# Two factor projections of a four-layer kernel: high and low halves of the weights side by side in one stationary tile

## The reference, cut to what matters

```
a = x @ Wa                      # [4, 512, 16]: one factor per token and head
b = x @ Wb                      # the same
for s in range(4):              # lags 0 to 3
    attn = einsum('bshd,bshd->bsh', q, lag(k, s)) * scale
    gate = sigmoid(lag(a, s) * b)
    out += (attn * gate)[..., None] * lag(v, s)
```

## Time and profile before

| | us |
|---|---|
| median of 3 runs | 2850.12 (2850.07 to 2850.35) |
| span of the profiled execution | 2847.8 |
| PE busy in that span | 2826.6 (99%) |
| DVE busy | 2252.7 (79%) |
| ACT busy | 1528.7 (54%) |
| POOL busy | 1443.2 (51%) |

### The profile page before, as it was taken

How to read it: one execution, slowest core, us unless ns; L and a number is a source line. 1 busy time by engine, 2 the same in 40 slices (tenths; PEclk the granted TensorE clock), 3 DMA queues, 4 the chain that set the end, 5 groups by cost and what they waited for, 6 DMA issues and landing times. The chain is left out here.

```text
span 2847.8 us, 40066 instructions
## 1 busy us (share of the span) xinstructions
PE 2826.6 (99%) x13466; PEld 2348.4 (82%) x13466; DVE 2252.7 (79%) x3265; ACT 1528.7 (54%) x3149; POOL 1443.2 (51%) x1016
## 2 busy tenths in 40 slices
PE   9999999999999999999999999999999999999998
PEld 7888888888788888888888888778778887888887
DVE  7899587777888889888988898977667677666665
ACT  6656333333666666666666666765545445444443
POOL 7787233334344444444444444666545556555554
PEclk9999999999999999999999999999999999999999
DMA  3000000000322222222222221321111111211111
GB/s 138 1 23 25 12 19 27 30 27 23 125 65 68 70 64 64 65 73 64 64 64 72 77 71 53 93 75 52 52 45 52 60 45 56 86 45 60 52 52 45
DMA packets 79099, 160.44 MB, mean 56 GB/s; under 512 B 11313, under 2 KB 19889, under 8 KB 77873
## 3 DMA queue, kind: packets, MB, share of 16 engines
q1 hardware_dynamic: 78896, 157.88, 18.5%
HBM read 115.63 MB, written 8.65 MB: 44 GB/s over the span
## 5 line engine op out<-in xcount | busy, mean ns | idle before, releaser
L1546 DVE SCALAR_TENSOR_TENSOR x_tok<-OP,expert_weight,x_tok 128x512 f32<-128x512 f32 x252 | 188.1, 748 | 138.2 <-PE OP L47 138.1
L1425 POOL TENSOR_TENSOR middle_w_lo<-second_raw,middle_w_hi 128x512 fp32r<-128x512 f32 (+1 forms) x96 | 143.4, 1496 | 208.7 <-ACT middle_w_hi L1420 208.7
L1518 POOL TENSOR_TENSOR middle_in_lo<-middle_slot,middle_in_hi 128x512 fp32r<-128x512 f32 x128 | 168.6, 1318 | 131.7 <-ACT middle_in_hi L1514 130.9
L3017 POOL TENSOR_TENSOR lag_rnorm<-lag_norm,minus_half 128x8 f32<-128x8 f32 x64 | 105.1, 1643 | 209.5 <-DVE lag_norm L3408 209.5
L45 PE MATMUL B<-xT_hi,lag_w_hi 128*128 128x512 f32 x516 | 201.4, 390 | 1.8 <-DVE xT_lo L496 1.5
L47 PE MATMUL B<-xT_hi,lag_w_lo 128*128 128x512 f32 x516 | 201.6, 391 | 0.0
L45 PE MATMUL A<-xT_hi,lag_w_hi 128*128 128x512 f32 x512 | 200.6, 392 | 0.4 <-DVE xT_lo L496 0.4
L46 PE MATMUL B<-xT_lo,lag_w_hi 128*128 128x512 f32 x516 | 200.8, 389 | 0.0
L47 PE MATMUL A<-xT_hi,lag_w_lo 128*128 128x512 f32 x512 | 199.9, 390 | 0.0
L46 PE MATMUL A<-xT_lo,lag_w_hi 128*128 128x512 f32 x512 | 199.4, 389 | 0.0
L45 PE MATMUL OP<-middle_down_hi,middle_in_hi 128*128 128x512 f32 x496 | 193.6, 390 | 1.9 <-POOL middle_down_lo L1445 1.7
(11 more groups left out here) (670 smaller groups left out, 9103.8 us busy)
## 6 DMA issues: line engine op xcount, KB each, us to landing
lag_raw<-in_head_weights SPq DMA_DIRECT2D x64, 256.0 KB, 4.5
lag_b_row<-lag_b_scratch SPq DMA_DIRECT2D x64, 256.0 KB, 3.3
lag_rot_q<-lag_r SPq DMA_DIRECT2D x128, 128.0 KB, 2.3
lag_rot_k<-lag_r SPq DMA_DIRECT2D x128, 128.0 KB, 2.4
middle_down_raw<-in_expert_down SPq DMA_DIRECT2D x32, 512.0 KB, 3.4
middle_raw<-in_expert_in SPq DMA_DIRECT2D x32, 384.0 KB, 3.0
second_raw<-in_expert_in SPq DMA_DIRECT2D x32, 384.0 KB, 3.0
double_raw<-in_dense_in SPq DMA_DIRECT2D x12, 512.0 KB, 3.4
```

Source lines behind the costliest of these rows:

```text
L1425: pool.tensor_tensor(self.w_lo[q % 2][:, out], self.raw[q % 2][:, of], f32(self.w_hi[q % 2][:, out]), ALU.subtract).then_inc(self.s_wlo, 1)
L1518: pool.tensor_tensor(self.inner_lo[q % 3][t], self.slot((1, 3)[t], q), f32(self.inner_hi[q % 3][t]), ALU.subtract).then_inc(self.s_lo, 1)
L1546: dve.scalar_tensor_tensor(row, self.down_bank(v, n), self.expert_weight[:, e:e + 1], row, op0=ALU.mult, op1=ALU.add).then_inc(self.s_acc, 1)
L3017: pool.tensor_tensor(rnorm[f.rbuf], norm2, half[:, 0:2 * TPB], ALU.pow).then_inc(s_rn, 1)
```

## The change

The factor weights are held once, doubled, instead of in two tiles. Columns 0 to 31 of each chunk are the high part of (Wa, Wb), columns 32 to 63 the low part, the rest zero (`GROUP` = 32). The same stationary tile is then multiplied with the high and with the low part of x: 8 matmuls per batch instead of 12. Rows 0 to 31 of the result hold the share of the high weights, rows 32 to 63 that of the low weights. The two halves are added in two ways. For a, `turn_row` uses `stacked`, a 128 x 16 tile with ones in rows i and 32 + i of column i, made once by DVE from the identity. For b, `store` writes the high half of 16 rows to the scratch (now 16 rows), and then a second DMA, issued by POOL with an adding write, adds the low half: `add_low(pool, b)`, which waits until the store has landed and the previous add is done. `row` of the next batch and every reader of the scratch now wait for the add (`s_added`) where they waited for the store.

```diff
     def split_lo(self, pool):
-        pool.wait_ge(self.s_hi, 1)
-        pool.tensor_tensor(self.w_lo, self.w_f, f32(self.w_hi), ALU.subtract).then_inc(self.s_lo, 1)
+        second = lambda t: t.rearrange("p (k n) -> p k n", n=P)[:, :, self.GROUP:2 * self.GROUP]
+        pool.wait_ge(self.s_r, 1)
+        pool.tensor_tensor(second(self.packed), second(self.w_f), f32(second(self.packed)),
+                           ALU.subtract).then_inc(self.s_lo, 1)
     def product_row(self, pe, b, bank=None):
-        product(pe, self.from_bank[b], [(self.w_hi[:, k * P:(k + 1) * P], self.w_lo[:, k * P:(k + 1) * P]) for k in range(KC)],
-                [(xT_hi[b][:, k, :], xT_lo[b][:, k, :]) for k in range(KC)]).then_inc(self.s_p, 1)
+        for k in range(KC):
+            w = self.packed[:, k * P:(k + 1) * P]
+            pe.matmul(self.from_bank[b], w, xT_hi[:, k, :], start=k == 0, stop=False)
+            done = pe.matmul(self.from_bank[b], w, xT_lo[:, k, :], start=False, stop=k == KC - 1)
+        done.then_inc(self.s_p, 1)
     def row(self, act, b):
         act.wait_ge(self.s_p, b + 1)
         if b:
             act.wait_ge(self.s_t, b)
-            if self.by_feature is not None:
-                act.wait_ge(self.s_out, 16 * b)
+            act.wait_ge(self.s_added, 16 * b)
         act.activation(self.rows, self.from_bank[b], ACT.Copy).then_inc(self.s_r, 1)
     def store(self, sp, b):
-        sp.wait_ge(self.s_r, b + 1)
-        sp.dma_start(self.by_feature[:, b * SEQ:(b + 1) * SEQ], self.rows[0:self.n, :]).then_inc(self.s_out, 16)
+        sp.wait_ge(self.s_r, b + 2)
+        sp.dma_start(self.place(b), self.rows[HEADS:self.GROUP, :]).then_inc(self.s_out, 16)
+
+    def add_low(self, pool, b):
+        pool.wait_ge(self.s_out, 16 * b + 16)
+        until(pool, self.s_added, 16 * b)
+        pool.dma_start(self.place(b), self.rows[self.GROUP + HEADS:2 * self.GROUP, :],
+                       accum_op=ALU.add).then_inc(self.s_added, 16)
     def turn_row(self, pe, b):
-            last = pe.matmul(self.turned[:, at:at + self.n_tok], self.rows[:, t * P:(t + 1) * P],
-                             self.mem["ident"][:, 0:self.n_tok], start=True, stop=True)
+            last = pe.matmul(self.turned[:, at:at + HEADS], self.rows[:, t * P:(t + 1) * P], self.stacked, start=True,
+                             stop=True)
@@ SP, in the slots
-                        sp.wait_ge(factors.s_out, 16)
+                        factors.stored(sp, 0)
                     else:
                         sp.wait_ge(s_gate, f.s)
                         if f.s < BATCH:
-                            sp.wait_ge(factors.s_out, 16 * f.s + 16)
+                            factors.stored(sp, f.s)
@@ POOL, in the slots
                     pool.tensor_tensor(r1, c1, cos, ALU.mult).then_inc(s_cos, 1)
+                    if f.s == 0:
+                        factors.add_low(pool, 0)
...
                     pool.tensor_tensor(squares[0], squares[0], squares[1], ALU.add).then_inc(s_pair, 1)
+                    if f.s == 0:
+                        factors.add_low(pool, 1)
                     pool.wait_ge(s_n2, f.s + 1)
                     pool.tensor_tensor(rnorm[f.rbuf], norm2, half[:, 0:2 * TPB], ALU.pow).then_inc(s_rn, 1)
+                    if f.s < 2:
+                        factors.add_low(pool, 2 + f.s)
@@ DVE, in the second layer
+                dve.wait_ge(pooled.s_small, 32)
+                dve.tensor_tensor(stacked, ident[:, 0:HEADS], ident[:, 2 * HEADS:3 * HEADS], ALU.add).then_inc(s_init, 1)
@@ program and kernel
-    lag_b = nc.dram_tensor("lag_b_scratch", [2 * HEADS, TOK], F32, kind="Internal").ap()
+    lag_b = nc.dram_tensor("lag_b_scratch", [HEADS, TOK], F32, kind="Internal").ap()
-        "head_factors": rows_first(padded(np.concatenate([v["L1_attn_Wa"], v["L1_attn_Wb"]], 1))),
+        "head_factors": rows_first(twice(np.concatenate([v["L1_attn_Wa"], v["L1_attn_Wb"]], 1))),
```

More of the change, by code:

```diff
@@ L1573, in again, with __init__ @@
         self.rows.high(act, 1, block)
[L1576 to L1583, removed]
+class Factors:
+    GROUP = 2 * HEADS
+    def __init__(self, nc, mem, w, by_token, w_f, packed, rows, banks, stacked, by_feature):
+        sem = Sems(nc, "factors")
+        self.mem, self.w, self.by_token, self.by_feature = mem, w, by_token, by_feature
+        self.w_f, self.packed, self.rows, self.stacked = w_f, packed, rows, stacked
         self.prod, self.turned = banks
         self.from_bank = {}
-        self.s_w, self.s_hi, self.s_lo = sem("w"), sem("hi"), sem("lo")
+        self.s_w, self.s_lo = sem("w"), sem("lo")
         self.s_p, self.s_r, self.s_t, self.s_c = sem("p"), sem("r"), sem("t"), sem("c")
-        if by_feature is not None:
-            self.s_out = sem("out")
+        self.s_out, self.s_added = sem("out"), sem("added")
     def load(self, sp):
@@ L1616, in row, with place, stored @@
             act.wait_ge(self.s_t, b)
[L1617 to L1618 removed]
+            act.wait_ge(self.s_added, 16 * b)
         act.activation(self.rows, self.from_bank[b], ACT.Copy).then_inc(self.s_r, 1)
+    def place(self, b):
+        return self.by_feature[:, b * SEQ:(b + 1) * SEQ]
     def store(self, sp, b):
[L1622 to L1623 removed]
+        sp.wait_ge(self.s_r, b + 2)
[5 more added lines that the diff above has]
+                       accum_op=ALU.add).then_inc(self.s_added, 16)
+    def stored(self, eng, b):
+        eng.wait_ge(self.s_added, 16 * b + 16)
     def turn_row(self, pe, b):
[L1626 to L1628 removed]
+        pe.wait_ge(self.s_r, b + 2)
+        until(pe, self.s_c, b)
         for t in range(TPB):
[L1630 to L1632 removed]
+            at = (b * TPB + t) * HEADS
+            last = pe.matmul(self.turned[:, at:at + HEADS], self.rows[:, t * P:(t + 1) * P], self.stacked, start=True,
+                             stop=True)
         last.then_inc(self.s_t, 1)
@@ L1636, in take @@
         dve.wait_ge(self.s_t, last + 1)
[L1637 to L1642, removed]
+        cols = slice(first * TPB * HEADS, (last + 1) * TPB * HEADS)
+        dve.tensor_scalar(self.by_token[:, cols], self.turned[:, cols], 0.5, None, ALU.mult).then_inc(self.s_c, 1)
 class Router:
@@ L1824, in layers @@
         MAT = KC * HID
-        small("spacing_of_rows", 336)
+        stacked = small("stacked", HEADS)
+        small("spacing_of_rows", 336 - HEADS)
         early = overlay("pool", [(f"{what}_{part}", MAT, F32R) for what in ("w_qa", "w_v", "w_ka", "m")
@@ L1912, in layers @@
         wo_hi, wo_lo = [lag["w_hi04"], lag["wo_hi1"]], [lag["w_lo04"], lag["wo_lo1"]]
-        factor_parts, factor_rows = (lag["w_hi05"], lag["w_lo05"]), start["factor_rows"]
+        factor_rows = start["factor_rows"]
         cos, sin, cross1, cross2, r1, r2 = (lag[n] for n in ("cos", "sin", "cross1", "cross2", "r1", "r2"))
@@ L2296, in _ @@
                         turn1.turn(pe, 1, [S0, S1, T, O], norm1.s_row)
+                        pe.wait_ge(s_init, 2)
                         factors.turn_row(pe, 0)
@@ L2671, in _ @@
                 act.wait_ge(s_tables, 48)
-                act.wait_ge(s_init, 2)
+                act.wait_ge(s_init, 3)
                 for f, l1, l2, l3 in slots():
@@ L3589, in rows_first, with twice @@
         return w.reshape(KC, P, -1).transpose(1, 0, 2).reshape(P, -1)
-    def padded(w):
-        return np.pad(w, ((0, 0), (0, P - w.shape[1])))
+    def twice(w):
+        return np.pad(np.concatenate([w, w], 1), ((0, 0), (0, P - 2 * w.shape[1])))
     def columns(t):
```

14 lines of the change are left out of this document (6 added, 8 removed).

## The result

The changed kernel takes 2856.49 us (median of 9 runs, 2854.92 to 2858.05), the kernel before 2850.22 (2850.07 to 2850.63) beside it. The ratio is 1.0023, 95% interval 1.0013 to 1.0033: 6.3 us slower. The profiled execution has a span of 2856.0 us against 2847.8, 8.2 us more; it is the second longest of the 9 runs.

The account below looks back on a forecast made before the run. Around the factor rows DVE, not PE, was taken as the tight engine. Two adds at 3.8 us less 3.7 us made +3.9 us: 2850.1 + 3.9 = 2854.0 us, range 2849.0 to 2860.5.

Parts of the forecast that it names:

- the bound to which I gave the larger chance: Whole kernel: the time stays within about 0.2% (5.7 us) of the kernel before; chance of same 0.63.
- The removed matmuls: PE's factor rows: 0.91 us saved per batch, worth 0 in batches 0 and 1, -0.91 us in full in batch 3.
- my last rival: PE's factor rows: matmuls could be slower with one stationary tile used twice in a row; no size or separate chance given.
- The chain: Slot 0: `row(1)` waits for add 0, `row(2)` for add 1, PE for that row; sum 2e - 3.7 us.
- The price e: Time of one adding DMA from POOL reaching it to the semaphore: 3.8 us taken, bounds 1.6 and 6.8.
- the dear case: Adding DMAs holding `row(1)` and `row(2)`: e over 4.7 us, slower by over 5.7 us; chance 0.28.
- The upper bound by a read after a write: Each add: reading the destination 3.3 us plus the slower store 3.5, in series 6.8, giving +9.9 us.
- Between row 1 and add 1: Slot 0: `store(1)` lands 3.3 us after `row(1)` starts, later than the sum of squares at 2.4.
- +4.8 until slot 1: PE, end of slot 0: slot 1 starts at about 776.9 in place of 772.15.
- For slot 1 I had -0.9: Slot 1: batch 3's four fewer matmuls on PE count in full, -0.91 us.
- DVE stretching the adds: POOL's adds beside a full DVE: 1.0 us more on each, e = 4.8, +5.9 us, 2856.0; chance 0.08.
- Adds 2 and 3: Later adds: add 2 covered by 2 us ahead of `row(3)`, add 3 holds POOL one or two us, no PE wait.

Follow-up runs that it names:

- experiment 1: The changed kernel without its adding DMAs, every wait for an add being a wait for the store again: 2849.16 us, ratio 0.9998.
- experiment 9: The kernel of experiment 7 with four matmuls that nobody reads between `turn_row(1)` and `product_row(2)`: 2847.62 us, ratio 0.9992.
- experiment 10: The kernel before the change with only PE's `turn_row(1)` moved ahead of `product_row(2)`: 2849.28 us against 2850.16, ratio 0.9997.
- experiment 5: The changed kernel with two buffers for the factor rows, so a row waits for the add of the batch before the last: 2851.47 us, ratio 1.0006.
- experiment 11: The kernel before the change, unchanged, profiled a second time: slot 0 starts at 745.74, span 2848.0 us.
- experiment 2: The changed kernel with the same four POOL DMAs as plain writes, without the addition: 2857.34 us, ratio 1.0025.
- experiment 4: The changed kernel with the next head's five loads moved ahead of store 1 on SP: 2852.24 us, ratio 1.0009.
- experiment 6: The changed kernel with 8 unread matmuls ahead of `product_row(1)` and 16 ahead of `turn_row(2)`, in PE's idle stretches: 2854.69 us, ratio 1.0017.
- experiment 7: The changed kernel with two row buffers, add 0 before the fourth root on POOL, and `turn_row(1)` ahead of `product_row(2)`: 2848.32 us, ratio 0.9994.
- experiment 8: The kernel of experiment 7 with the next head's five loads also moved ahead of store 1: 2848.92 us, ratio 0.9995.

## Why the prediction was right and where it was wrong

The direction, the place and the chain of waits held, and the range (2849.0 to 2860.5) held the time; it was 11.5 us wide. The likeliest value (2854.0) was 2.5 us too low, and the result, 0.22% slower, lies just beyond the bound to which I gave the larger chance. That it was no further off is in part luck: in the profile, errors of -1.2 and -0.8 us stand against +2.5 and +3.0, and the last is of a mechanism that I did not have. Step by step:

- *The removed matmuls.* 8 matmuls per row at 0.23 us. The savings of batches 0 and 1 went into PE's wait for DVE, 1.46 to 3.00 us, as said. That of batch 2 shows in experiment 1 (0.92 us). Batch 3's is in slot 1's length there (16.76 us, not 17.65). Together they are the 1.82 us of experiment 1's profile. In the medians they arrive only in part there (1.1 us); experiments 9 and 10 agree with the value (2.5 less 0.9 leaves 1.6) but do not prove it, since 9 differs in more than this. That one stationary tile used twice in a row is slower, my last rival, is refuted: 8 matmuls take 1.8 us at the full clock.
- *The chain.* `row(1)` and `row(2)` wait for the adds, and PE for `row(2)`. Experiment 5 takes the buffer's reuse away and the waits with it; experiment 1 shows that little else is lost, the open 0.4 us ahead of slot 0 apart (experiment 11).
- *The price e*, the mis-sized term. I put 3.8 on each. From POOL reaching it to ACT's start, add 0 took 2.6 and add 1 6.3 us: the first 1.2 less, the second 2.5 more. With no loads or save in flight at its issue, a DMA of 32 KB from POOL lands after 1.9 to 2.1 us when plain (experiment 2) and after 2.3 to 2.6 when adding. I had named the loads as an argument for the dear case, and then gave both adds the same price, though in my own chain these loads were issued ahead of add 1. The upper bound by a read after a write was the wrong mechanism: the addition costs 0.4 us (experiment 2), the loads beside it 3.8 (experiment 4).
- *Between row 1 and add 1* I had 3.3 us by the store; it took 2.5 by the sum of squares. The store had landed first.
- *What I did not have at all: the clock.* I wrote that the matmuls run at 1.00 and let every idle stretch cost only its own length. The lower clock added 0.9 us in `turn_row(2)` (1.73 for 0.82) and 2.1 in slot 1's first projection (4.98 for 2.84), 3.0 us together. That these count is borne out by experiment 4, where they are gone with the long wait, and by experiment 6, which leaves the waits and fills them. The half-speed `product_row(2)` (3.23 us for 8 matmuls, not 1.82) was hidden, since PE waited for `row(2)` behind it anyway. In the span's account: I had +4.8 until slot 1; add 0 -1.2, add 1 +2.5, the gap -0.8 and the clock +0.9 make +6.2, measured +6.1. For slot 1 I had -0.9; with the clock's 2.1 that is +1.2, measured +1.3.
- *DVE stretching the adds.* Not seen. Add 0 was issued beside a full DVE (2.00 of the 2 us from 764 to 766) and was the quick one. Add 1 was issued at 770.26, while DVE was idle until 770.67; DVE worked until 772.90 and was idle again for the last 3.6 us of the add (0.00 us from 774 to 776). The Trainium skill's rule on GpSimd's descriptors and VectorE's two-port mode ("SBUF — State Buffer", section "SBUF: two separate sides") does not explain the slow add. The Trainium skill's fit of 2.0 us plus bytes over 436e3 ("DMA: Bandwidth & Descriptors", section "Anatomy of one DMA — SWDGE (gpsimd) path") agrees with the undisturbed ones: the estimate for 32 KB is 2.1 us, measured are 1.9 to 2.1 plain and 2.3 to 2.6 adding. It has no term for a neighbour, and with loads in flight 5.8 to 6.5 were measured.
- *Adds 2 and 3.* As said, hidden: `row(3)` at 790.17 shows no wait. POOL waited 5.82 us for store 2 and 0.80 for store 3, with no engine waiting for POOL behind that.

## What to carry to other kernels

Removing work on an engine that is 99% busy gains nothing where it waits a moment later (batches 0 and 1 here), and a new DMA in a chain of buffer reuse is paid with its whole latency each time round; a second buffer (here in room that the change itself had freed) or an issue in an idle place takes it off. Price a small DMA by what is in flight when it is issued, and not by its size alone. And when a stall on PE is forecast, price the work behind it at both clocks: the matmuls that follow can run at half speed.

## What the runs showed of the hardware that I had not expected

- PE's granted clock fell to 0.50 behind idle stretches of 3.0 and 4.4 us, and also behind two waits of 1.0 and 0.9 us with a short turn between them (experiments 7 and 8) and behind waits of 1.19, 0.16 and 0.80 us (experiment 6); not behind 1.46 us in the kernel before, nor behind 0.22, 0.65 and 0.69 us (experiment 4). It is not the same each time: behind the same 2.98 us it stayed at 1.00 in experiment 1 and fell for about 7 us in experiment 5.
- Useless matmuls in an idle stretch kept the clock up and lowered the median by 1.8 us (experiment 6). In experiment 9 four of them kept it up in the profile, and the median was 0.7 us lower, which the spread of the runs could also give.
- An adding DMA of 32 KB from POOL occupied it for 0.8 to 1.0 us (a plain one 0.55 to 0.73) and landed 2.3 to 2.6 us after its issue with no loads or save in flight then, 5.8 to 6.4 beside 1.25 MB of loads. A store of the same 32 KB by SP took 1.6 us, and 4.8 beside loads and save (experiment 8).
